# Attention rounds of a fused transformer kernel: q and k of both token tiles projected in one step and v later, and the summing, squaring and scaling of the head outputs on GpSimd

## The reference, cut to what matters

```
q = (x @ Wq.T + bq).reshape(B, S, H, 2 * hd)      # k alike; v has hd columns for each head
q1, q2 = rope(q[..., :hd]), rope(q[..., hd:])     # k1, k2 alike
a1 = softmax(causal(q1 @ k1.T * scale)); a2 = softmax(causal(q2 @ k2.T * scale))
out = (a1 - lam * a2) @ v
out = out * rsqrt(mean(out * out, -1) + EPS)      # over the 8 values of one head
return (out * head_norm_w * (1 - LAMBDA_INIT)) @ Wo.T + bo
```

## Time and profile before

| | us |
|---|---|
| median of 3 runs | 1374.61 (1374.16 to 1375.39) |
| the profiled execution, its own time | 1372.76 |
| its span in the trace | 1371.0 |
| attention rounds, first maximum to last exponential of the 19 rounds | about 312 to 843 in the trace |

### The profile page before, as it was taken

One profiled execution on the slowest core, in us unless ns is written; L12 is line 12 of the kernel. 1 busy time (PEld: TensorE's weight loads), 2 busy tenths in 40 slices (PEclk: granted clock), 3 DMA queues, 4 the chain that ended last, 5 costly groups with the idle time before them and its releaser, 6 DMA issues. The chain is left out here.

```text
span 1371.0 us, 33098 instructions
## 1 busy us (share of the span) xinstructions
PE 1083.3 (79%) x11600; PEld 783.0 (57%) x11600; DVE 952.3 (69%) x2490; ACT 708.2 (52%) x1359; POOL 805.2 (59%) x1058
## 2 busy tenths in 40 slices
PE   3555777646999999898999896687787497999787
PEld 1324656524766666666666664466665274666556
DVE  7546545446788898989898974475555784778662
ACT  4522434334766777777776764333344364444164
POOL 5754555522666667777777766514555233888751
PEclk9766999878999999999999998689999699999989
DMA  8113222122111111111221110422221400000001
GB/s 253 47 36 93 82 75 71 38 86 52 46 43 43 38 37 46 45 45 45 50 51 48 38 34 17 133 67 68 70 65 36 127 1 1 0 1 1 1 23 40
DMA packets 92561, 71.73 MB, mean 52 GB/s; under 512 B 39408, under 2 KB 81808, under 8 KB 91760
## 3 DMA queue, kind: packets, MB, share of 16 engines
q1 hardware_dynamic: 82960, 48.58, 13.5%
q0 software_dynamic: 9440, 21.02, 4.5%
HBM read 30.19 MB, written 24.17 MB: 40 GB/s over the span
## 5 line engine op out<-in xcount | busy, mean ns | idle before, releaser
L2096 DVE TENSOR_REDUCE diff_peak<-diff_s_ps 128x2 f16<-128x512 f32 (+1 forms) x384 | 257.4, 684 | 55.6 <-PE diff_s_ps L2373 28.2
L1953 ACT ACTIVATE diff_prob<-diff_st_ps 128x512 f32<-128x512 f32 x384 | 225.7, 598 | 122.2 <-PE diff_st_ps L2398 117.5
L1869 POOL TENSOR_SCALAR_AFFINE_SELECT diff_prob<-diff_prob 128x256 f32<-128x256 f32 (+1 forms) x384 | 188.1, 496 | 133.4 <-ACT diff_prob L1953 128.3
L433 POOL DMA_INDIRECT exp_ys<-moe_y_sb,moe_dest x156 | 158.2, 1014 | 173.4 <-ACT moe_y_sb L516 137.1
L2398 PE MATMUL diff_st_ps<-diff_qT,diff_k_one 128*128 128x256 f16 (+1 forms) x1024 | 147.1, 247 | 5.1 <-DMA diff_qT<-diff_peakT 4.7
L2421 PE MATMUL diff_ot_ps<-diff_prob,diff_v 128*32 128x128 f32 x3072 | 124.7, 280 | 8.2 <-POOL diff_prob L1869 5.0
L503 ACT ACTIVATE moe_act<-moe_g_ps 128x512 f32<-128x512 f32 x94 | 55.3, 588 | 122.5 <-remote 87.9
L509 ACT ACTIVATE moe_h_hi<-moe_h 128x512 f16<-128x512 f32 x94 | 59.2, 630 | 91.7 <-DVE moe_h L741 78.3
L722 DVE COPY moe_xgT<-moe_t_ps 128x512 f16<-128x512 f16 x78 | 32.8, 420 | 97.7 <-PE moe_t_ps L945 78.6
L2373 PE MATMUL diff_s_ps<-diff_k_one,diff_qT 128*128 128x256 f16 x512 | 99.6, 277 | 0.0
L2421 PEld LDWEIGHTS diff_ot_ps<-diff_prob,diff_v 128*32 128x32 f32 x3072 | 72.7, 109 | 43.2 <-issue 22.3
(11 more groups left out here) (406 smaller groups left out, 3042.7 us busy)
## 6 DMA issues: line engine op xcount, KB each, us to landing
moe_xg<-exp_xs SPq DMA_DIRECT2D x78, 130.0 KB
diff_k_one<-diff_kT SPq DMA_DIRECT2D x128, 64.0 KB, 2.0
diff_qT<-diff_peakT SPq DMA_DIRECT2D x256, 1.0 KB
diff_yg<-exp_ys SPq DMA_DIRECT2D x14, 256.0 KB
fetched_yg<-exp_ys SPq DMA_DIRECT2D x7, 512.0 KB, 4.3
diff_k_tri<-diff_kT SPq DMA_DIRECT2D x64, 50.0 KB
diff_q_tri<-diff_qT SPq DMA_DIRECT2D x64, 50.0 KB
exp_ys<-moe_y_sb,moe_dest POOLq DMA_INDIRECT x156
```

The lines of the kernel that those rows point to most:

```text
L433: nc.gpsimd.indirect_dma_start(out=ew.ys, out_offset=bass.IndirectOffsetOnAxis(ap=dest[:, s, j:j + 1], axis=0), in_=y_sb[:, s % YR, j], in ...
L1869: nc.gpsimd.affine_select(out=pr, in_=pr, compare_op=ALU.is_ge, fill=0.0, base=0, pattern=[[0, n], [1, P]], channel_multiplier=-1).then_in ...
L1953: nc.scalar.activation(prob[:, u % RING], st_ps[:, u % 2], ACT.Exp, scale=SCALE).then_inc(exp_ready, 1)
L2096: nc.vector.tensor_reduce(to, s_ps[:, u % 2].rearrange("p (m k) -> p m k", m=n), op=ALU.max, axis=AX.X, negate=True).then_inc(max_ready, 1)
```

## The change

- TensorE at step 7 projects q and k of both tiles: four products of 256 columns, each of three matmuls. They fill both banks of `m_ps`. At step 11, when both rotations are done, it projects v of both tiles, two products of 128 columns. The transposes of k's packs move from step 15 to 14, ahead of the output projection.
- VectorE rotates at steps 7 and 9 and takes k's rests tile by tile at 12 and 13. The sum, the square and the scaling leave it. It sums and averages the squares at steps 8 and 20 (`mean_squares`).
- GpSimd sums and squares at steps 6 and 18, adds the rotated parts at 8 and 10, and then at step 10 polishes and scales. It adds the second fetched result at step 5 instead of 6, and takes q's rests at 17 and 18.
- ScalarE guesses at step 9 instead of 8, copies v in one piece at 12, k into the packs at 10 and 12 and q at 16 and 17. The normalised x of even rounds is made at steps 8, 9 and 11, and its upper half at 13 instead of 16; GpSimd's power for it moves from step 6 to 5, VectorE's shift from 9 to 7.

```diff
-    ADD_AT = (3, 6)
+    NORMALISE_AT = {8: (0,), 9: (1, 2), 11: (3,)}
+    ADD_AT = (3, 5)
...
+            def combine(b, half):
+
+                pool.wait_ge(o_weighted, b * 2 + half + 1)
+                if half == 0 and not below(b, 1):
+                    pool.wait_ge(onT_in_psum, b)
+                heads = slice(8 * half, 8 * half + 8)
+                om, sq = o[:, :, heads], osq[:, :, heads]
+                nc.gpsimd.tensor_tensor(om, weighted[:, :, :, 0], weighted[:, :, :, 1], ALU.add).then_inc(o_summed, 1)
+                pool.wait_ge(o_summed, b * 2 + half + 1)
+                nc.gpsimd.tensor_tensor(sq, om, om, ALU.mult).then_inc(o_squared, 1)
...
+            def scale_outputs(b):
+
+                pool.wait_ge(rms_ready, b + 1)
+                nc.gpsimd.tensor_tensor(on[:].rearrange("p j h d -> p (j h) d"), o[:].rearrange("p j h d -> p (j h) d"),
+                                        rms[:].rearrange("p j h -> p (j h)").unsqueeze(2).broadcast_to([P, 2 * HEADS, HD]),
+                                        ALU.mult).then_inc(on_ready, 1)
...
-                        if u == 14:
-                            wait_apart(pool, pack_hi, A * 4 + 4, made)
-                            for j in range(2):
-                                last = nc.gpsimd.tensor_tensor(q_pack[:, j, :, HD:2 * HD], rot[:, j, 0:MAPS],
...
+                        if u in (17, 18):
+                            j = u - 17
+                            wait_apart(pool, pack_hi, A * 4 + 3 + j, made)
+                            nc.gpsimd.tensor_tensor(q_pack[:, j, :, HD:2 * HD], rot[:, j, 0:MAPS],
+                                                    q_pack[:, j, :, 0:HD], ALU.subtract).then_inc(pack_lo_q, 1)
...
-                        if u in (9, 12):
-                            j = (u - 9) // 3
+                        if u in (8, 10):
+                            j = (u - 8) // 2
                             pool.wait_ge(rope_taken, A * 2 + j + 1)
...
                             nc.gpsimd.tensor_tensor(rot[:, j], by_cos[:, j], by_sin[:], ALU.add).then_inc(rot_ready, 1)
...
-                    if D is not None and u == 8:
+                    if D is not None and u == 6:
+                        combine(D, 1)
+                    if C is not None and u == 18:
+                        combine(C, 0)
+                    if D is not None and u == 10:
                         rms_of(D)
+                        scale_outputs(D)
...
-                        if u in (10, 11):
-                            normalise(norms, (0, 1) if u == 10 else (2, 3))
-                        if u == 16:
-                            a.wait_ge(n_xn_ready, 2 * norms + 2)
+                        if u in NORMALISE_AT:
+                            normalise(norms, NORMALISE_AT[u])
+                        if u == 13:
...
-                        if u in (9, 12):
-                            j = (u - 9) // 3
-                            a.wait_ge(rope_taken, A * 2 + j + 1)
+                        if u == 12:
+                            a.wait_ge(v_in_psum, A + 1)
...
+                            nc.scalar.activation(v_new[:].rearrange("p j h d -> p (j h d)"), m_ps[:, 0, 0:S], ACT.Copy).then_inc(v_taken, 1)
+                        if u in (16, 17):
+                            j = u - 16
+                            src = rot[:, j, 0:MAPS].unsqueeze(2).broadcast_to([P, MAPS, 2, HD])
+                            dst = q_pack[:, j].rearrange("p m (r d) -> p m r d", d=2 * HD)[:, :, :, 0:HD]
+                            nc.scalar.activation(dst, src, ACT.Copy).then_inc(pack_hi, 1)
+                        if u in (10, 12):
+                            j = (u - 10) // 2
                             a.wait_ge(rot_ready, A * 2 + j + 1)
...
-                            dst = q_pack[:, j].rearrange("p m (r d) -> p m r d", d=2 * HD)[:, :, :, 0:HD]
-                            nc.scalar.activation(dst, src, ACT.Copy).then_inc(pack_hi, 1)
...
+                d_step.k = 2 * half
+                if not below(b, 1) or half:
+                    dve.wait_ge(o_squared, b * 2 + half)
...
-            def combine(b, half):
-
-                dve.wait_ge(o_weighted, b * 2 + half + 1)
...
+            def mean_squares(b, half):
+
+                dve.wait_ge(o_squared, b * 2 + half + 1)
...
-                d_step(nc.vector.tensor_tensor(om, both[:, :, :, 0], both[:, :, :, 1], ALU.add))
-                d_step(nc.vector.tensor_tensor(sq, om, om, ALU.mult))
-                d_step(nc.vector.tensor_reduce(ms[:, :, heads], sq, op=ALU.add, axis=AX.X))
+                d_step(nc.vector.tensor_reduce(ms[:, :, heads], osq[:, :, heads], op=ALU.add, axis=AX.X))
                 nc.vector.tensor_scalar(ms[:, :, heads], ms[:, :, heads], 1.0 / HD, RMS_EPS, ALU.mult, ALU.add).then_inc(ms_ready, 1)
...
-                dve.wait_ge(qkv_in_psum, A * 2 + j + 1)
-                qk = m_ps[:, :, 0:QK].rearrange("p b (m d) -> p b m d", d=HD)
-                if j:
-                    dve.wait_ge(rot_ready, A * 2 + 1)
+                    dve.wait_ge(pack_lo, A * 2)
+                    dve.wait_ge(pack_lo_q, A * 2)
+                dve.wait_ge(qk_in_psum, A + 1)
+                qk = m_ps[:, :, j * QK:(j + 1) * QK].rearrange("p b (m d) -> p b m d", d=HD)
...
+                if j:
+                    dve.wait_ge(rot_ready, A * 2 + 1)
...
-                    if D is not None:
-                        if u == 10:
-                            dve.wait_ge(rms_ready, D + 1)
-                            nc.vector.tensor_tensor(on[:].rearrange("p j h d -> p (j h) d"), o[:].rearrange("p j h d -> p (j h) d"),
-                                                    rms[:].rearrange("p j h -> p (j h)").unsqueeze(2).broadcast_to([P, 2 * HEADS, HD]),
-                                                    ALU.mult).then_inc(on_ready, 1)
...
-                        if u in (8, 11):
-                            rotate(A, (u - 8) // 3)
-                        if u == 14:
-                            dve.wait_ge(pack_hi, A * 4 + 4)
...
+                        if u in (7, 9):
+                            rotate(A, (u - 7) // 2)
+                        if u in (12, 13):
+                            j = u - 12
+                            dve.wait_ge(pack_hi, A * 4 + 1 + j)
+                            nc.vector.tensor_tensor(k_pack[:, j, :, 2 * HD:3 * HD], rot[:, j, MAPS:],
+                                                    k_pack[:, j, :, 0:HD], ALU.subtract).then_inc(pack_lo, 1)
                     if D is not None:
                         if u == 6:
                             weigh(D, 1)
-                            combine(D, 1)
+                        if u == 8:
+                            mean_squares(D, 1)
                             d_step.end()
...
-                    if C is not None and u == 19:
-                        combine(C, 0)
+                    if C is not None and u == 20:
+                        mean_squares(C, 0)
...
+
+            def project(out, j, cols):
+                for i, (xt, wt) in enumerate(((xT_hi, wqkv_hi), (xT_hi, wqkv_lo), (xT_lo, wqkv_hi))):
+                    last = nc.tensor.matmul(out, xt[:, j * P:(j + 1) * P], wt[:, cols], start=(i == 0), stop=(i == 2))
+                return last
...
-                    if u in (7, 10) and A is not None:
-                        j = (u - 7) // 3
+                    if u == 7 and A is not None:
                         pe.wait_ge(xT_ready, A + 1)
...
-                        if j == 1:
-                            pe.wait_ge(rope_taken, A * 2 + 1)
-                            pe.wait_ge(v_taken, A * 2 + 1)
-                        else:
...
-                                pe.wait_ge(o_weighted, D * 2 + 2)
...
+                        if C is not None:
+                            pe.wait_ge(peakT_ready, C * 3 + 3)
+                        if D is not None:
+                            pe.wait_ge(o_weighted, D * 2 + 2)
+                        for j in range(2):
+                            for part in range(2):
+                                last = project(m_ps[:, part, j * QK:(j + 1) * QK], j, slice(part * QK, (part + 1) * QK))
+                        last.then_inc(qk_in_psum, 1)
+                    if u == 11 and A is not None:
+                        pe.wait_ge(rope_taken, A * 2 + 2)
+                        for j in range(2):
+                            last = project(m_ps[:, 0, j * P:(j + 1) * P], j, slice(2 * QK, QKV))
+                        last.then_inc(v_in_psum, 1)
                     if u == 13 and D is not None:
                         pe.wait_ge(on_ready, D + 1)
                         if A is not None:
-                            pe.wait_ge(rope_taken, A * 2 + 2)
+                            pe.wait_ge(v_taken, A + 1)
                         for j in range(2):
...
-                    if A is not None and u in (15, 22):
-
-                        h4 = 0 if u == 15 else 4
```

(7 more changed lines are left out.)

52 lines of the change are left out of this document (16 added, 36 removed).

## The result

| | before | changed |
|---|---|---|
| median of the runs | 1374.38 us (1370.77 to 1375.39, 4 runs) | 1384.97 us (1380.46 to 1388.49, 4 runs) |
| ratio, 95% interval | | 1.008 (1.0051 to 1.0109) |
| profiled execution, span | 1372.76, 1371.0 | 1380.46, 1378.6 |
| from the first copy of x to the last x addition | 564.18 | 576.18 |

A forecast was written before the change was run, and what follows sets the result against it. Attention rounds were taken as bound by TensorE and VectorE handing each other buffers. 13 x 0.88 + 0.9 + 1.2 - 0.6 = 12.9 us gave 1385.7 profiled, 1387.5 median; range 1380 to 1393 (0.50), 8 in 10 1366 to 1399.

The forecast's parts named there:

- the last rounds: Rounds at the end without batch A; only the last round was costed, ending 0.9 us later.
- 13 full rounds: Rounds 3 to 15, with all four batches; each 0.88 us longer, mean of odd 1.06 and even 0.7.
- round 0: First attention round; q's copies now stand behind that of k's transposes, costing 1.0 to 1.3 us, 1.2 in the sum.
- rounds 1 and 2: Early rounds lacking a stage; the early rotation may give back 0.3 us each, 0.6 in the sum.
- The rotations and the means: VectorE, steps 7 to 9: GpSimd's addition holds up the mean, costing 0.5 us a round; second rotation ends 1.4 earlier.
- W: End of the division of D's outputs in a round, the zero from which the prediction counts times.
- What takes the place of the wait: GpSimd adds, polishes, scales after the second rotation; TensorE waits 0.9 us for scaled outputs, step 16 1.06 later (odd round).
- The even round: Round without routing product, with ScalarE's normalised x ahead of the guess; forecast 0.7 us longer.
- the transposes of q: TensorE's transposes of tile 1 of q at step 20, close to q's rests; 0 to 0.3 us.
- Rival (a), faster: GpSimd keeps up, TensorE's queue gets no new wait at the scaled outputs: 13 x -0.65 us, 1366 us; chance 0.23.
- Rounds with one end missing: Rounds lacking a stage: last round +0.9 us, round 0 +1.0 to 1.3, rounds 1 and 2 -0.3 each.
- Covered, at no cost: GpSimd's sum and square at step 6 end long before the mean; without that cover 1 us a round.

The follow-up runs named there:

- second pair: Traces of the kernel before and the changed kernel, both run again unchanged on the follow-up chips; 1261.49 and 1277.88 us.
- mean_early: Changed kernel with VectorE's sum and mean of D's squares at step 7, ahead of the first rotation, not at step 8; 1269.78 us, ratio 1.0052.
- after_again: The changed kernel, unchanged, run again on the follow-up chips; 1277.88 us, ratio 1.0101 to the kernel before.
- proj_only: Changed kernel with sum, square and scaling back on VectorE and guess and polishing at step 8, leaving the projection part; 1270.68 us, ratio 1.0058.
- scale_vector_mean: mean_polish_early with the scaling alone back on VectorE, at step 10, in all rounds; 1254.90 us, ratio 0.9915 to the kernel before.
- before_again: The kernel before, unchanged, run again on the follow-up chips; 1261.49 us, ratio 0.9987.
- mean_polish_early: Changed kernel with means at step 7, guess at 8, polishing and scaling on GpSimd at 9, between its two rotated additions; 1261.51 us, ratio 0.9984.
- after_tail: Changed kernel with the last three rounds' sums, squares and scaling back on VectorE, guess and polishing there at step 8; 1271.26 us, ratio 1.0051.
- gpsimd_only: Kernel before plus the GpSimd part alone: sum, square, scaling on GpSimd, later means and guess, polishing at step 10, old projection; 1270.49 us, ratio 1.0053.
- the last run: scale_vector_mean with the last three rounds' sums and squares also back on VectorE, on a chip of the first kind; 1364.5 us, ratio 0.9913.

## Why the prediction came out, point by point

**The time.** 1387.5 was forecast, 1384.97 measured. That the two are 2.5 us apart is in part luck. The profiled execution, for which 1385.7 was forecast, took 1380.46, as the part outside the attention was 4.4 us shorter in it. And of the terms of the sum two are wrong in opposite ways, the full rounds too dear by 3 us and the last rounds too cheap by 2.4 and 5.3:

| term | forecast | first pair of traces | second pair |
|---|---|---|---|
| 13 full rounds | +11.4 | +8.5 | +8.2 |
| the last rounds | +0.9 | +3.3 | +6.2 |
| round 0 | +1.2 | +2.3 | +1.6 |
| rounds 1 and 2 | -0.6 | -2.1 | -0.2 |
| sum | +12.9 | +12.0 | +15.7 |

**The rotations and the means: right.** The means have a median of 395 ns, 175 before. The median mixes the means of both halves; that of step 8, which the prediction is about, takes 0.60 to 0.61 us in all 13 full rounds and ends 0.03 after the addition in each:

```profile
L2145 DVE TENSOR_SCALAR diff_ms<-diff_ms x32: 174/395/607, 364.0 to 860.0; 128x16 f32<-128x16 f32 x32
```

So the hold costs 0.43 us, for 0.5 forecast. The prediction read "623 ns once" from its row, which shows only the longest: in the kernel before 5 of the 13 full rounds, all even, have a mean of 0.60 to 0.62 us, beside another addition. mean_early took the mean out of there and the full rounds fell by 7.5 us, 0.6 a round; that is more than the hold, for the reduce of 0.28 us and the mean's own 0.17 left the chain with it. The second rotation was forecast to end at W + 6.53 and ended at W + 6.39. VectorE's idle time ahead of the cosines, "about 1 us", was 1.15, and 11.1 us in 11 waits in the 330 to 710 us of after_again.

The shared port of the Trainium skill ("SBUF — State Buffer", section "Who interferes with whom") also bears on what I hadn't costed, VectorE's scaling in proj_only: its 1.12 us beside GpSimd's addition against 0.41 agree with that rule. In scale_vector_mean VectorE is the first to begin (581.96, the addition 582.20), and there it is the addition that is stretched, 1.45 us for 1.27. That is 0.18 us, where the two overlap for 0.32, so that the second one is blocked in full isn't seen from this side. The scalings have a mean of 572 ns there; they begin beside a causal cut of GpSimd's.

**What takes the place of the wait: right in kind, a little too dear.** Scaled outputs transposed at W + 9.95 forecast, W + 9.78 measured; TensorE there at W + 9.0, measured W + 9.0; idle time 0.9 forecast, 0.78 measured, within the 0.7 to 1.2 named as the sign. k's transposes have no wait, as forecast. Step 16 at W + 13.5 forecast, W + 13.25 measured: +0.81 us in the odd round for +1.06, and the full rounds show +0.65 in the mean (8.2 us over 405.66 / 32.2 = 12.6 rounds) for 0.88. Of the 0.25 us too many, 0.14 are the second rotation, 0.1 the scaling (0.73 us by the addition of 128x256, it took 0.63), and 0.08 the part behind the wait; the polishing took 0.1 more, 1.32 us for 1.22.

**The even round: the term that was mis-sized.** 0.7 us was forecast for it. In the two traces of the changed kernel TensorE transposes the scaled outputs at W + 9.78 in even rounds as in odd ones, with the same wait of 0.78, so the 0.2 us for ScalarE's normalisation ahead of the guess never came. Step 16 starts at W + 12.95 in each even round, against W + 12.84 in all but the first before: 0.11 us later. From one division to the next the even rounds grew by 0.28 us in the mean (0.46 in the second pair of traces), the odd ones by 1.11 (0.88). So the odd round was about right and the even one less than forecast, which is most of the 3 us. And a part of what the even rounds did lose lies where the prediction had allowed 0 to 0.3 us and put nothing into the sum, at the transposes of q, here in after_again:

```profile
604.60 0.62 PE L2637 MATMUL diff_m_ps<-diff_ident_h,diff_q_pack 128*128 128x128 f16 x8 [0.43 <-POOL diff_q_pack L1902]
...
606.82 0.62 PE L2637 MATMUL diff_m_ps<-diff_ident_h,diff_q_pack 128*128 128x128 f16 x8 [0.54 <-POOL diff_q_pack L1902]
```

Three of its even rounds have both of these waits on GpSimd's rests of q; before_again has 0.22 us at the first, for the division, and none at the second.

**Rival (a), faster.** It needed a wait under 0.2 us, and the waits are 0.78. With another order on GpSimd and VectorE such a kernel exists: mean_polish_early has no such wait in its full rounds, and they are 5.8 us shorter than before (the rival had said 8.5). The order on GpSimd's queue, named as the evidence against it, was the right evidence.

**Rounds with one end missing: the step that failed most.** I costed only the last round, and as a chain of its own lengths (+0.9). In the last round alone it was about right: 0.5 us and 1.1 (23.95 against 23.49, 24.27 against 23.20). The loss is in the one ahead of it, where I had set nothing: 26.79 against 24.03 and 27.03 against 21.87. The prediction counted the additions that the polishing is moved past in GpSimd's queue, but not the scatters, which in round 17 also stand at step 10, nor the slower clock after a wait of 2.5 us. after_tail shows that this term was GpSimd's: all but 0.6 us of it is gone (74.10 against 73.53) when VectorE has the work.

**Round 0.** 2.3 and 1.6 us for 1.0 to 1.3. The time of this round moves by as much between kernels in which round 0 has the same instructions (22.26, 22.51, 24.87), so it can't be told how far off this is.

**Covered, at no cost: half right.** The sums and squares at step 6 are hidden, as said. But in gpsimd_only VectorE's relief of 1.7 us a round (336.6 and 316.3 us of busy time from 330 to 710) bought 0.2 us over all full rounds. Not because nothing had waited for it: the first rotation came 0.74 us earlier, and the guess, which waits for the later mean with ScalarE's copy of v behind it, gave that back. The prediction's "only where VectorE is what TensorE waits for" leaves out this case, in which TensorE waits for two engines and the change relieves one and delays the other. Whether the GpSimd part can gain by itself isn't shown; the two fastest kernels have its sums and squares in the full rounds, but together with the new projection and other places.

## What to carry to other kernels

Moving work off a busy engine pays only if its end is waited for, and if the one that waits isn't held by another engine that the same change delays: list all that the waiting instruction waits for. When a chain runs VectorE, GpSimd, VectorE, GpSimd through one buffer, the best place for work added to the second engine was, here, the gap in which the other engine works for it. With the means out of the way each time, polishing and scaling gave 406 us for the full rounds behind both additions, 400 between them, and 414 ahead of both (in the order of projections of the kernel before). And read the rounds that lack a stage, and even and odd ones, on their own: what is hidden in the full round may be the bound there.

## What the runs showed that I had not expected

- The same kernel took 1374 to 1377 us in the first measurement and on the chip of the last run, and 1261 to 1265 us on the three chips between. 103 of the 111 us of span lie outside the attention (806.8 and 703.6 us), which itself took 564.2 and 556.3; what makes them isn't known. The ratios are alike on both: 1.008 and 1.0101 for the changed kernel, 0.9915 and 0.9913 for the two best.
- A single wait of 2.52 us of TensorE, in a round in which it is busy for 21 of 27 us, was followed by a granted clock of 0.50 for the rest of the round: the same group of matmuls 1.08 us against 0.65. The scale of the loss (5.2 us in that round for 2.5 of waiting) couldn't be told from the idle time alone.
- An instruction of VectorE that begins beside GpSimd's addition ended 0.28 us after it when it had 128x256 elements (begun 0.43 us into it in proj_only, 1.03 in the odd rounds of before_again), and 0.03 after it with 16 values (all 13 full rounds of the changed kernel): its place in time is set by the other engine's end.
